# Attention and routed experts on one core: `finish()` inside the branch arms, 16-bit marks with column pairs innermost, sums by a scan, and another table of expert tiles

## What is computed

```python
xn = _layernorm(x, axis=-1)
x = x + attn(xn, W_q, W_k, W_v, W_o) + ffn(xn, Wg, gamma, beta, W1, b1, W2, b2)

# attn, H = 16 heads of DK = 8
Q, K, V = apply_rope(proj(W_q)), apply_rope(proj(W_k)), proj(W_v)
attn = softmax(Q @ K.T / sqrt(DK))
out = (attn @ V) @ W_o.T
# ffn, E = 8 experts, D = 128, F = 512
scores = xf @ Wg
w, idx = top_k(scores, 2);  w = softmax(w)
normed = xhat * gamma[e] + beta[e]
h = relu(normed @ W1[e] + b1[e])
out[e] = h @ W2[e] + b2[e] + xf
y = sum over the two chosen experts of w * out[e]
```

## Time and profile before

| | |
|---|---|
| median of the runs | 587.76 us |
| the profiled execution | 589.15 us, span 587.2 us |
| PE busy | 541.0 us, 92% |
| ACT busy | 501.4 us, 85% |
| DVE busy | 300.9 us, 51% |
| GpSimd busy | 246.0 us, 42% |
| chain that ended last, by engine | PE 63%, ACT 21%, DVE 8%, issue 3% |

### The profile page before, as it was taken

One profiled execution on the slowest core, in us unless ns is written; L12 is line 12 of the kernel. 1 busy time (PEld: TensorE's weight loads), 2 busy tenths in 40 slices (PEclk: granted clock), 3 DMA queues, 4 the chain that ended last, 5 costly groups with the idle time before them and its releaser, 6 DMA issues.

```text
span 587.2 us, 12446 instructions
## 1 busy us (share of the span) xinstructions
PE 541.0 (92%) x4620; PEld 246.0 (42%) x4620; DVE 300.9 (51%) x1002; ACT 501.4 (85%) x552; POOL 246.0 (42%) x303
## 2 busy tenths in 40 slices
PE   8899988878999999999899999999989999999783
PEld 6323312222455554445345555434534555554111
DVE  4975789965434344463344433555433444343672
ACT  2699999989898788898888888899899888888992
POOL 4299900078646444556223444365521444322000
PEclk9999999999999999999999999999999999999996
DMA  7144320051435545324443464433433455460821
GB/s 257 29 138 123 113 62 11 1 181 49 159 108 165 185 149 162 99 75 149 136 133 105 163 211 153 141 100 100 160 98 114 154 176 188 142 188 30 315 81 39
DMA packets 44657, 75.47 MB, mean 129 GB/s; under 512 B 7585, under 2 KB 17873, under 8 KB 44081
## 3 DMA queue, kind: packets, MB, share of 16 engines
q1 hardware_dynamic: 39232, 63.71, 33.9%
q0 software_dynamic: 4544, 9.32, 5.2%
q10 hardware_dynamic: 816, 1.61, 0.7%
HBM read 33.88 MB, written 8.85 MB: 73 GB/s over the span
## 4 chain that ended last, share of the span: by engine, by line
PE 63%; ACT 21%; DVE 8%; issue 3%; DMA 2%; POOL 1%; SPq 1%; ACTq 1%; another core or an unknown queue 0%; POOLq 0%; DVEq 0%
PE acc L696 29%; ACT ring L921 20%; PE sc L661 11%; PE aside_bank L740 9%; PE sc L754 8%; PE aside_bank L768 2%; DMA sin<-rope_sin 2%; DVE xn L1228 2%; PE aside_bank L572 1%; PE sc L729 1%; DVE xn L1230 1%; DVE xn L1233 1%; PE aside_bank L588 1%; DVE blocks L1089 1%; SPq L332 1%
## 5 line engine op out<-in xcount | busy, mean ns | idle before, releaser
L921 ACT ACTIVATE ring<-sc 128x1024 f32<-128x1024 f32 x512 | 488.0, 1040 | 59.9 <-PE sc L661 55.9
L696 PE MATMUL acc<-ring,v 128*9 128x512 f32 x2048 | 250.9, 595 | 18.3 <-ACT ring L921 11.8
L513 POOL DMA_INDIRECT work<-normed,token x71 | 71.3, 1004 | 235.1 <-DVE work L1290 181.5
L661 PE MATMUL sc<-qs,ks 32*128 32x512 f16 x1024 | 101.4, 384 | 16.2 <-ACT ring L921 14.1
L1296 DVE TENSOR_SCALAR work<-aside_bank,xn 128x128 f32<-128x128 f32 x216 | 60.8, 345 | 107.1 <-PE aside_bank L740 105.8
L661 PEld LDWEIGHTS sc<-qs,ks 32*128 32x128 f16 x1024 | 26.2, 91 | 177.5 <-ACT ring L921 150.6
L696 PEld LDWEIGHTS acc<-ring,v 128*9 128x9 f32 x2048 | 39.9, 89 | 117.0 <-issue 76.5
L523 POOL DMA_INDIRECT token_out<-work,token x71 | 69.8, 983 | 37.6 <-issue 19.2
L740 PE MATMUL aside_bank<-work,xn 128*128 128x128 f32 x432 | 62.6, 288 | 0.0
L740 PEld LDWEIGHTS aside_bank<-work,xn 128*128 128x128 f32 x432 | 52.3, 191 | 12.2 <-issue 12.2
L754 PE MATMUL sc<-xn,work 128*128 128x128 f32 x432 | 57.2, 275 | 0.0
(11 more groups left out here) (194 smaller groups left out, 416.4 us busy)
## 6 DMA issues: line engine op xcount, KB each, us to landing
xn<-w_rest SPq DMA_DIRECT2D x54, 323.0 KB
xn<-L_ffn_W SPq DMA_DIRECT2D x54, 256.0 KB
w_last<-w_rest SPq DMA_DIRECT2D x17, 323.0 KB
w_last<-L_ffn_W SPq DMA_DIRECT2D x17, 256.0 KB
qs<-hl SPq DMA_DIRECT2D x60, 64.0 KB
ks<-hl SPq DMA_DIRECT2D x60, 64.0 KB
x<-L_attn_x SPq DMA_DIRECT2D x4, 512.0 KB, 8.2
w_rest<-L_ffn_W SPq DMA_DIRECT2D x8, 256.0 KB, 4.0
```

Of the source, the lines that this page charges most:

```text
L513: pool.indirect_dma_start(out=xt[t % TILE_BUFFERS], out_offset=None, in_=xh_d[:, :], in_offset=bass.IndirectOffsetOnAxis(ap=token[:, 0, t: ...
L661: last = nc.tensor.matmul(dst, ks[r:r + 32, kb * P:(kb + 1) * P], qs[r:r + 32, at], start=True, stop=not slow)
L696: last = nc.tensor.matmul(acc[32 * j:32 * j + VW, :], v9[:, b, kb, 4 * g + j, :], ring[:, (2 * n + j // 2) % UNITS, j % 2, :], start=(kb = ...
L921: nc.scalar.activation(ring[:, (2 * n + u) % UNITS, :, :], sc[HOME[2 * n + u]][:, :].rearrange("p (h c) -> p h c", h=2), ACT.Exp, scale=SC ...
```

## The change

Tables: marks move from steps 32 to 44 to steps 26 to 34, the inversion from 35 to 47 to steps 29 to 36, tokens from 47 to 36, owners from 29 to 37, the projections of batch 1 to steps 38, 40, 46 and 50. Tiles now have the even steps from 42 to 238 instead of 52 to 236, which leaves five free steps more than tiles need. `SECOND_PAIRS` takes steps 64, 104, 140, 178 and 216: there, layer one of a tile is in the free pair before and layer two and the transpose in this one, in `aside_bank` and not in a spare score buffer. `ONE_AT` says in which step a layer one is, `TWO_AT` in which a layer two; `BOTH` has the 66 steps with both.

```diff
-ROUTE_AT, RANKS_AT, SLOTS_AT, OWNER_AT, GATES_AT = 21, 24, 24, 29, 39
-INVERT_AT = {n: g for g, n in enumerate((35, 37, 38, 40, 43, 44, 46, 47))}
-MARK_AT = {n: g for g, n in enumerate((32, 33, 35, 37, 40, 41, 43, 44))}
-TOKENS_AT = 47
-PLAIN_AT = {n: (1, r) for r, n in enumerate((28, 49, 50, 54))}
+ROUTE_AT, RANKS_AT, SLOTS_AT, OWNER_AT, GATES_AT = 21, 24, 24, 37, 43
+INVERT_AT = {n: g for g, n in enumerate(range(29, 29 + GROUPS))}
+MARK_AT = {n: g for g, n in enumerate((26, 27, 29, 30, 31, 32, 33, 34))}
+TOKENS_AT = 36
+PLAIN_AT = {n: (1, r) for r, n in enumerate((38, 40, 46, 50))}
...
-NORM_AT = {PER_BATCH * b - 6: b for b in range(1, B)}
+NORM_AT = {PER_BATCH * b - 8: b for b in range(1, B)}
...
+FFN_FROM, FFN_TO = 42, 240
+FREE = [n for n in PAIRS if n not in TAKEN]
+MORE = len(FREE) - (SLOT_TILES + 1)
...
-SQUARE_AT.update({n: (1, r) for r, n in enumerate((53, 55, 56, 57))})
+SQUARE_AT.update({n: (1, r) for r, n in enumerate((43, 45, 50, 54))})
...
-MERGE_AT = {LOAD_AT + 4 + 3 * b: b for b in range(B)}
+MERGE_AT = {LOAD_AT + n: b for b, n in enumerate((4, 6, 9, 10))}
...
+        def tile_home(n):
+            return sc[SPARE[n]] if n in BOTH else aside_bank
...
+            def tiles_are_taken(n):
+                wait(pe, tile_taken, len([m for m in TWO_AT if m < n]))
...
             def layer_two_and_turn(k, n):
-                home = sc[SPARE[n]]
-                pe.wait_ge(e_ok, SPARE_NEED[n])
+                home = tile_home(n)
+                if n in BOTH:
+                    pe.wait_ge(e_ok, SPARE_NEED[n])
+                else:
+                    pe.wait_ge(bank_taken[0], USE["second", k])
...
             def aside(n):
+                tiles_are_taken(n)
                 if n == WO_AT:
                     turn_wo()
...
+                if n in ONE_AT:
+                    layer_one(ONE_AT[n])
+                if n in TWO_AT:
+                    layer_two_and_turn(TWO_AT[n], n)
...
                     if b + 1 < B:
                         batches(b + 1, following)
+                    else:
+                        finish()
                 with pe.Else():
                     for later in range(b, B):
                         attend(later, True)
+                    finish()
+
+            def finish():
+                weigh(STEPS - 1)
+                project_out(B - 1, 1)
 
             batches(0, flag_of(0))
-            weigh(STEPS - 1)
-            project_out(B - 1, 1)
```

```diff
-                    v.wait_ge(xh_out, 16 * B)
+                    v.wait_ge(indices_ok, 3)
...
-                nc.vector.tensor_tensor(place_mark[k], iota_p.unsqueeze(1).to_broadcast([P, GROUP, P]),
-                                        slot_hl[:, 1, js].unsqueeze(2).to_broadcast([P, GROUP, P]), ALU.is_equal)
...
+                tiles, places = [P, GROUP // 2, SLOT_TILES, 2], [P, GROUP // 2, P, 2]
+                link(nc.vector.tensor_tensor(tile_mark[k], all_tiles.unsqueeze(1).to_broadcast(tiles),
+                                             of_columns(slot_hl[:, 0, :], tiles), ALU.is_equal))
+                nc.vector.tensor_tensor(place_mark[k], all_places.unsqueeze(1).to_broadcast(places),
+                                        of_columns(slot_hl[:, 1, :], places), ALU.is_equal)
+                nc.vector.tensor_scalar(named[k][:, :, 0, :, :], tile_mark[k], row_name, None, ALU.mult)
+                nc.vector.tensor_tensor(named[k][:, :, 1, :, :], tile_mark[k], of_columns(pick_16, tiles), ALU.mult
                                         ).then_inc(mark_ok, 1)
...
+                link(nc.vector.tensor_tensor_scan(upto, not_first, totals, 0.0, ALU.mult, ALU.add))
```

More of the change, by code:

```diff
@@ L130, in bank_uses @@
             ("turn", TURN_AT), ("values", VALUES_AT), ("invert", INVERT_AT), ("plain", PLAIN_AT), ("norm", NORM_AT),
-            ("bound", FLAG_AT), ("out", PROJECT_AT), ("one", TILE_AT)) if n in at and at.get(n) != SLOT_TILES]
+            ("bound", FLAG_AT), ("out", PROJECT_AT), ("one", ONE_AT)) if n in at]
         pieces += [(name,) for name, at in (("wo", WO_AT), ("rows", COLUMNS_AT), ("ranks", RANKS_AT),
@@ L136, in bank_uses @@
             take(0, *piece)
+        if n in TWO_AT and n not in ONE_AT:
+            use["second", TWO_AT[n]] = count[0]
     take(0, "out", B - 1, 1)
@@ L151, in score_homes @@
             order = [2] + order
-        before = n - 2 if n - 2 in TILE_AT else None
+        before = n - 2 if n - 2 in BOTH else None
         for u in range(2):
@@ L213, in build @@
         pick = work[:, 4 * T * E:6 * T * E].rearrange("p (a t e) -> p a t e", a=2, e=E)
-        rank = work[:, 6 * T * E:8 * T * E].rearrange("p (a t e) -> p a t e", a=2, e=E)
+        behind = work[:, 6 * T * E:7 * T * E].rearrange("p (t e) -> p t e", e=E)
+        totals, not_first = (work[:, k * T * E:(k + 1) * T * E] for k in (7, 8))
         turned = [sb(f"turned{k}", [P, CH]) for k in range(4)]
@@ L218, in build @@
         const = sb("const", [P, 5 * P + 2 * T])
-        ident, before = const[:, 0:P], const[:, P:2 * P]
+        ident, not_before = const[:, 0:P], const[:, P:2 * P]
         head_row = const[:, 2 * P:2 * P + 2 * H]
@@ L671, in maxima @@
                 wait(pe, e_ok, 2 * PER_QUAD * q)
-                wait(pe, tile_taken, len([n for n in TILE_AT if n < PER_QUAD * q]))
+                wait(pe, tile_taken, len([n for n in TWO_AT if n < PER_QUAD * q]))
                 pe.wait_ge(m_wide[b], 2 * (base + 1))
@@ L713, in ranks @@
                 enter_bank(0, "ranks")
-                nc.tensor.matmul(bank[0][:, 0:T * E], before, cnt[:, 0, :, :], start=True, stop=True)
+                nc.tensor.matmul(bank[0][:, 0:T * E], not_before, cnt[:, 0, :, :], start=True, stop=True)
                 nc.tensor.matmul(bank[0][:, T * E:2 * T * E], ones[:, :], cnt[:, 0, :, :], start=True, stop=True
@@ L721, in invert @@
                 for i in range(GROUP):
-                    last = nc.tensor.matmul(bank[0][:, 0:2 * SLOT_TILES], place_mark[g % 2][:, i, :],
-                                            named[g % 2][:, i, :, :].rearrange("p v c -> p (v c)"),
+                    last = nc.tensor.matmul(bank[0][:, 0:2 * SLOT_TILES], place_mark[g % 2][:, i // 2, :, i % 2],
+                                            named[g % 2][:, i // 2, :, :, i % 2].rearrange("p v c -> p (v c)"),
                                             start=(i == 0), stop=(i == GROUP - 1))
@@ L821, in attend @@
                         pe.wait_ge(e_ok, NEED[2 * n + 3])
-                        if n - 2 in TILE_AT:
-                            pe.wait_ge(tile_taken, TILE_AT[n - 2] + 1)
+                        if n - 2 in BOTH:
+                            pe.wait_ge(tile_taken, TWO_AT[n - 2] + 1)
                     for u in range(2):
@@ L1150, in take_ranks @@
                 bank_is_full(0, "ranks")
-                nc.vector.tensor_copy(rank[:, :, :, :], bank[0].rearrange("p (a t e) -> p a t e", a=2, e=E)
+                nc.vector.tensor_copy(totals.rearrange("p (e t) -> p t e", e=E),
+                                      bank[0][:, T * E:2 * T * E].rearrange("p (t e) -> p t e", e=E))
+                nc.vector.tensor_copy(behind, bank[0][:, 0:T * E].rearrange("p (t e) -> p t e", e=E)
                                       ).then_inc(bank_taken[0], 1)
@@ L1329, in aside @@
                     take_sums(n // KB - 1)
-                if TILE_AT.get(n, SLOT_TILES) < SLOT_TILES:
-                    relu(TILE_AT[n])
-                if n in TILE_AT:
-                    rows_and_columns(TILE_AT[n], n)
+                if n in ONE_AT:
+                    relu(ONE_AT[n])
+                if n in TWO_AT:
+                    rows_and_columns(TWO_AT[n], n)
                 if n % KB == 0 and n > 0:
```

108 lines of the change are left out of this document (52 added, 56 removed).

## The result

The changed kernel takes 608.75 us, median of four runs (606.85 to 609.34); the kernel before took 586.2 beside it. The ratio is 1.0393, with a 95% interval of 1.036 to 1.0426: slower by 22.6 us. The forecast was 614, range 606 to 630. The profiled execution has a span of 607.4 us.

The account below looks back on a forecast made before the run. Neither PE nor ACT alone bounds it: a tight 4.58 us tile-pair loop, where delayed values delay both. Terms +34.3 - 2.7 - 1.6 - 1.0 - 3.0 = +26.0, on the median of 587.76 about 614 us, range 606 to 630.

Parts of the forecast that it names:

- wait behind whole tiles, and behind layer-two pairs: PE's values wait for DVE's tile_taken: +34.3 us over 66 whole-tile pairs; a wait of 0.54 in each layer-two pair.
- split without its wait: Five tiles split over two pairs, since a whole tile costs 0.91 us: -2.7, and -2.8 more without the layer-two wait.
- the end: Last values and projection, issued before PE's branch out of the arms: -3.0 us, bounds -1.5 and -3.65.
- setup: Steps 24 to 52, marks and inversion: 2.4 us lost against ACT's pace instead of 4.0, so -1.6.
- squares: ACT's squares for batch 1: two of them fall in ACT's idle of a tile pair, -1.0 us.
- 66 x 0.52: 66 pairs with tile and spare buffer, times the mean wait of PE's values for DVE, 0.52 us: +34.3 us.
- The rival in which DVE is late in every pair: The values' wait in every tile pair is as long as in the pair shown: +54 instead of +34.3, 634 us; 10%.
- PE's share between 180 and 540 us: Sign expected in the new profile's steady stretch: PE's busy share falls to about 88%.
- half, by the nearest row: DVE's marks: 16-bit two-source instructions take half the time, so a mark takes 1.74 us instead of 2.87.
- the marks stay at 2.87: Rival on DVE's marks in the setup: they get no faster, +7.5 us, 622 us; 15%.
- the ledger of DVE: DVE work in steps 29 to 34, 13.2 us against ACT's 11.0: step 32's transpose is late, values wait about 1.7.
- The -0.9: Part of the end: PE's idle gap shrinks, the full clock may last, and the last projection gains 0.9 us.

Follow-up runs that it names:

- e1: The changed kernel with PE's wait for tile_taken at the head of aside only in even steps; 577.36 us, ratio 0.9863 to the kernel before.
- e5: e1 with no tile split, whole tiles in even steps from 42 to 228, which also starts DVE's merges ten steps earlier; 583.59 us, ratio 0.9967.
- e4: e1 with the last values and last projection moved back behind PE's arms, as in the kernel before; 580.53 us, ratio 0.9935.
- e2: The kernel before with only the wait for tile_taken added at the head of PE's aside; 614.93 us, ratio 1.0509.
- e3: e1 with the odd step's wait put back, but between the even step's values and the odd step's; 577.15 us, ratio 0.9869.
- e8: The changed kernel with a fifth 128x128 DVE instruction behind each tile's four relus, written to an unread tile; 624.06 us, ratio 1.0663.
- e9: The changed kernel with e1's even-step wait and e8's fifth DVE instruction behind the relus; 577.24 us, ratio 0.9872.
- e10: e1 with the slots kept in float32, so each mark's two comparisons have one 32-bit operand; 583.6 us, ratio 0.9973.
- e6: e1 with tiles from step 44 instead of 42, so four tiles are split instead of five; 576.71 us, ratio 0.9857.
- e7: e1 with marks and inversions spread over later steps, tokens a step later and tiles from step 44; 578.77 us, ratio 0.9895.

## Why the prediction was right, and where its terms were off

The prediction's terms, with what the runs measured. Differences are by ratios times 585 us, where a row doesn't say otherwise.

| term | predicted | measured | from |
|---|---|---|---|
| wait behind whole tiles, and behind layer-two pairs | +34.3 +2.8 = +37.1 | +31.0 | changed kernel against e1 |
| split without its wait (-2.7 -2.8) | -5.5 | -6.1 | e1 against e5 |
| the end | -3.0 | -3.2 (medians), -4.2 (ratios) | e1 against e4 |
| setup -1.6, squares -1.0 | -2.6 | +1.3 to +2.3 | what is left of e1's -8.0 |
| sum | +26.0 | +22.6 to +23.0 | |

The ratios have intervals of 0.9 to 1.9 us to either side, so the fourth row, a remainder of three of them, is good to about 2.5 us. No run measured the squares by themselves.

**The wait: right place and mechanism, 6 us too dear.** e1 takes the loss away, e2 brings it back alone, e3 shows that the same wait later is free, and e8 with e9 that it is DVE's chain that PE waits for. What was mis-sized is the term 66 x 0.52. The 0.52 was the mean over the tiles of before, among them many like the earlier trace rows, where the relus started late (1.54 us behind layer one). I compared, tile by tile, when the first relu starts behind the first matmul of layer one: over 1.35 us in 23 of 71 tiles of before, but in none of e2, one of the changed kernel and one of e1. With prompt relus a tight pair costs 0.47, and 66 x 0.47 = 31.0. That was the lower bound named, and it should have been the value: the drift is no property of the wait. Nor is it one of the tight pace, since e1 runs at 4.59 us a pair without it. The rival in which DVE is late in every pair is refuted by the same count. Layer-two pairs I had at 4.13; the pair at step 64 of the changed kernel reads

```profile
159.79 0.39 PE L698 MATMUL sc<-qs,ks 32*128 32x512 f16 x4
...
162.04 1.91 PE L733 MATMUL acc<-ring,v 128*9 128x512 f32 x16 [0.34 <-DVE work L1323]
163.88 0.39 PE L698 MATMUL sc<-qs,ks 32*128 32x512 f16 x4
```

and takes 4.09 from scores to scores, where 3.67 is free.

Pair by pair, from scores to scores, the traces of the changed kernel and of e1 close the account. The 65 whole pairs behind the first take 5.06 us on average instead of 4.62, 28.4 in all. The six layer-two pairs take 4.04 instead of 3.77, 1.6 in all and not 2.8, since some of them had a stall of their own without the wait. The pair at step 42 takes 5.99 instead of 5.23. Layer-one pairs and pairs without a tile are the same to 0.2 us in all. That is 30.6 of the 30.9 us.

One sign was misjudged: PE's share between 180 and 540 us, forecast at about 88%, is 92%.

**Splits.** 5.5 against 6.1 by the ratios, but 1.9 of the traces' 5.2 lies where e5 moves the merges, so the close match is in part luck: the pairs themselves are worth 3.3 to 3.9 in the traces. The idea behind the term held: a pair costs 4.58 only if both layers stand in it, and either alone fits under ACT's 3.67 (the layer-one and layer-two pairs of e1 take 3.67 to 3.99, but for the one at step 42).

**Marks.** The step "half, by the nearest row" gave 1.74 us for a mark. DVE's timeline of the changed kernel, against the earlier trace rows:

```profile
80.15 0.45 DVE L1262 TENSOR_TENSOR xn<-xn,slot_hl 128x568 bf16<-128x568 bf16 x1
80.64 0.69 DVE L1264 TENSOR_TENSOR xn<-xn,slot_hl 128x1024 bf16<-128x1024 bf16 x1
...
81.53 0.45 DVE L1267 TENSOR_TENSOR xn<-xn,pick 128x568 bf16<-128x568 bf16 x1
81.89 0.45 DVE L1262 TENSOR_TENSOR xn<-xn,slot_hl 128x568 bf16<-128x568 bf16 x1
```

80.15 to 81.89 is 1.74 exactly. The Trainium skill, "VectorE: DVE Perf Modes", section "What auto-detection actually checks", states this rate for two-source instructions whose tensors are all 16-bit with step 1; the rows agree. The rule that the Trainium skill gives in "Vector Engine (DVE) Microarchitecture Reference", section 5.2, and that I had left out of the sum, would by the prediction's estimate have made a mark 0.7 us longer. With one word, a pair of 16-bit values, read again and again, no such loss shows: the row has 0.69 for 1024 elements. The rival "the marks stay at 2.87" was priced at +7.5; e10 comes nearest to it, with marks of 2.57 us and +6.4.

**The setup: the term that was wrong.** I had steps 24 to 52 losing 2.4 us against ACT's pace, where before they lost 4.0. In the changed kernel steps 24 to 42 alone take 36.74 us (the exponentials of step 24 start at 70.35, those of step 42 at 107.09) for 18 x 1.83 = 32.9, a loss of 3.8 (e1 takes the same 36.74); the kernel before took 33.58 for the same steps and lost its time behind them. In e1, which has the same stage without the wait on whole tiles, steps 42 to 52 take 23.48, where three pairs with a tile and two without come to 3 x 4.58 + 2 x 3.67 = 21.1. So e1 loses 3.8 + 2.4 = 6.2 us between steps 24 and 52 where 2.4 was forecast, and that is the step of the prediction that failed. Three waits of PE make most of it:

```profile
82.03 0.69 PE L759 MATMUL aside_bank<-xn 128*128 128x142 bf16 x8 [0.69 <-DVE xn L1267]
90.22 1.05 PE L733 MATMUL acc<-ring,v 128*9 128x512 f32 x8 [1.58 <-DVE blocks L1132]
108.76 0.33 PE L766 MATMUL aside_bank<-const,work 128*128 128x128 f32 x1 [1.70 <-DVE rotated L1305]
```

The second is the one I had worked out, 1.7 by the ledger of DVE and 1.58 in the row. Beside it, an inversion step runs at 1.93 us, not 1.83, for PE's own scores, multiplication and values add up to 0.33+0.62+0.98; I had costed DVE alone there. The third stands behind step 42's scores, where the first tile now begins while DVE still has the rotations of the projections just ahead of it. I had given the first tile's start nothing and considered only gathers and weights for it; it was DVE's queue. In some executions it has a second price, in the granted clock. Windows of the changed kernel (PE clock is the last but two):

```profile
70.00:107.00 37.00, 32.54 (x292) 9.29 (x288) 33.40 (x92) 34.62 (x38) 10.36 (x15) 1.00 0.24 68
...
110.00:113.40 3.40, 3.37 (x21) 2.09 (x17) 0.94 (x4) 2.46 (x3) 2.98 (x3) 0.50 0.62 226
```

From 110.0 to 113.4 the clock is at the lower level, 1.2 GHz, after PE had idled 1.70 us; layer one takes 2.08 us there instead of 1.16. e1, e4 and e9 have the same wait and a clock of 0.50 behind it. But e3, e5, e8 and e10 have the same wait too, and there the clock stays at 1.00. PE in e3:

```profile
108.40 0.33 PE L766 MATMUL aside_bank<-const,work 128*128 128x128 f32 x1 [1.71 <-DVE rotated L1307]
...
109.96 1.16 PE L777 MATMUL aside_bank<-work,xn 128*128 128x128 f32 x8
...
112.06 0.40 PE L698 MATMUL sc<-qs,ks 32*128 32x512 f16 x4 [0.83 <-ACT ring L966]
```

So the idle time alone doesn't bring the clock down; what else it takes is not shown. The price can be read: steps 42 to 52 take 23.48 us in e1 and 23.50 in e4, 22.85 in e3 and 22.84 in e5, so the low clock costs 0.6 us. It isn't half of the 3.4 us, since at the full clock PE waits 0.83 us for ACT in that place. e6, which starts tiles at 44, has neither that wait nor a slow layer one.

**The end: right in sum, one of three parts left to the execution.** The last values start 0.05 us behind the last exponential and take 1.05 instead of 1.70, both as forecast. But the projection, forecast at 1.2 us, still takes 2.07 in the profiled execution, at the lower clock, behind 2.20 us in which PE is idle for DVE's transposes and division. The last rows of PE in the changed kernel, and behind the dots the projection in e3:

```profile
598.87 1.05 PE L733 MATMUL acc<-ring,v 128*9 128x512 f32 x8 [0.70 <-ACT ring L964]
602.12 2.07 PE L803 MATMUL aside_bank<-woT,oT 128*128 128x128 f32 x8 [2.20 <-DVE oT L1142]
...
570.30 1.16 PE L803 MATMUL aside_bank<-woT,oT 128*128 128x128 f32 x8 [2.20 <-DVE oT L1144]
```

From the last exponential to the end it is 8.5 us (598.82 to 607.35), against 11.3 before: 2.8 less. The two parts that came were forecast at 2.1 + 0.65 = 2.75. The -0.9 came in other executions: behind the same 2.20 us of idle the projection takes 2.07 or 2.08 in the profiles of the changed kernel, e1 and e5, 1.28 in e7, and 1.16 in those of e3, e6, e8, e9 and e10, where the time from the last exponential to the end is 7.6 us. The part was right as a possibility and wrong as a certainty.

**How the 5.25 us between forecast and median close.** 1.6 are not the change's: the ledger stood on a median of 587.76, and the kernel before took 586.2 beside the changed one (584.66, 585.43 and 584.68 in the three groups). In the remaining 3.7 errors of both signs cancel: 6.1 too much for the wait, 0.6 too little gained by the splits, 0.2 to 1.2 too little by the end, and some 4 too little lost in the setup. That the cause and its size were found is no luck; that the sum lay within 1% of the median is in part. The gain of e1, -8.0 where the sum without the wait said -11.1, shows the setup's error without the wait's in front of it.

## What to carry to other kernels

A semaphore wait costs by where it stands in the waiter's queue: follow the chain that gives the semaphore to its end, and put the wait directly ahead of the first instruction that needs it. Here it stood one phase early, up to 0.47 us a pair on an engine without idle time, 31 us in all. When a per-tile wait is priced from a trace in which the releaser is sometimes late for reasons of its own, take the prompt tiles for the value and the mean for the upper bound. When work is drawn forward to the first step at which its inputs exist, look at what every engine's queue still holds then, not at the inputs alone.

## What was not expected of the hardware

**Stretched instructions on DVE.** DVE's timeline of the changed kernel, and GpSimd's at the same time:

```profile
105.33 1.93 DVE L1139 TENSOR_TENSOR att<-blocks,rec 128x128 f32<-128x128 f32 x1
107.30 0.75 DVE L1006 SCALAR_TENSOR_TENSOR turned<-aside_bank,gain,cos 128x512 f32<-128x512 f32 x1
...
105.82 1.28 POOL L531 TENSOR_TENSOR turned<-turned,rotated 128x512 f32<-128x512 f32 x1
```

The product of two tensors takes 0.29 us elsewhere and 1.93 here. It ends at 107.26, 0.16 behind GpSimd's two-source instruction, which ends at 107.10. The product is stretched to 1.92 to 1.94 us in all nine traces in which it begins shortly before this instruction of GpSimd, and ends 0.16 behind it in each. In e7 DVE's L1007 is stretched likewise, from 0.75 to 2.47, and ends 0.56 behind the same instruction of GpSimd. That one has two inputs in SBUF; the form of it that reads `aside_bank` in PSUM keeps its 0.75 in all 14 places where it runs beside GpSimd's. That DVE is held up by GpSimd fits all these rows, but no run moved the one to free the other, and by its usual length the product would have ended at 105.62, 0.2 us before the recorded start of GpSimd's instruction; spans on GpSimd are rough. The Trainium skill, "GPSIMD Engine Reference", section 1, states that GpSimd's SBUF interfaces are shared with VectorE and contended by DVE instructions with two SBUF inputs, which the product is; the trace agrees, with 1.93 us beside GpSimd's instruction and 0.29 elsewhere. These 1.6 us lie in front of the shuffle that the first tile waits for.

**Late relus in one execution.** In the profiled execution of before, relus drift up to 0.8 us behind their usual place in stretches of consecutive tile pairs; in e2, the same kernel with one wait more, they never do. That execution took 589.15 us, where the medians were near 585. Whether it was that execution or the old order of work at full pace stays open: before was profiled once.
